# Projecting the later batches beside the attention heads, in one straight program

## What is computed

```python
Q, K, V = (proj(Wq, bq), proj(Wk, bk), proj(Wv, bv))        # [B, H, N, dh]
S = jnp.einsum('bhnd,bhmd->bhnm', Q, K) / dh ** 0.5
W_tau = jax.nn.softmax(S, axis=-1)
W_sigma = 1.0 / ((1.0 + jnp.abs(S) / b_) ** 2 + t_ ** 2)
W_sigma = W_sigma / W_sigma.sum(axis=-1, keepdims=True)
f = 0.5 * tau + 0.5 * sigma        # tau = W_tau @ V, sigma = W_sigma @ V, heads side by side
y = f @ Wo.T + bo
out = x + ln_w * (y - mu) * jax.lax.rsqrt(var + LN_EPS) + ln_b
```

## Time and profile before

| | before |
|---|---|
| median of 3 runs | 2139.07 us (2138.07 to 2139.43) |
| the profiled execution, its own time | 2139.67 us |
| its span, first to last instruction | 2137.9 us |
| granted TensorE clock, mean | 0.911 |
| first sigma scores of head 0 | 96.27 us |
| last instruction of attend_heads | 1699.8 us |
| PE busy | 1622.2 us (76%) |
| VectorE busy | 1888.1 us (88%) |
| ScalarE busy | 1577.8 us (74%) |
| GpSimd busy | 1609.9 us (75%) |

### The profile page before, as it was taken

One profiled execution on the slowest core, in us unless ns is written; L12 is line 12 of the kernel. 1 busy time (PEld: TensorE's weight loads), 2 busy tenths in 40 slices (PEclk: granted clock), 3 DMA queues, 4 the chain that ended last, 5 costly groups with the idle time before them and its releaser, 6 DMA issues. The chain is left out here.

```text
span 2137.9 us, 34185 instructions
## 1 busy us (share of the span) xinstructions
PE 1622.2 (76%) x8579; PEld 574.7 (27%) x8579; DVE 1888.1 (88%) x3699; ACT 1577.8 (74%) x1395; POOL 1609.9 (75%) x1198
## 2 busy tenths in 40 slices
PE   4477777878777778878777877777777668798976
PEld 2211222212211212222121212112221234366655
DVE  5799999999999999999999999999999378755556
ACT  3288889988888998989898998898998611122243
POOL 2399999999999999999999999999999321100000
PEclk9689999999999999999999999999999878877788
DMA  3300000000000000000000000000000000000001
GB/s 104 103 7 12 12 11 11 15 13 11 11 11 11 15 13 11 11 11 12 14 13 11 11 11 12 14 13 11 11 11 11 1 1 0 1 0 0 0 1 40
DMA packets 28864, 31.75 MB, mean 15 GB/s; under 512 B 5210, under 2 KB 16545, under 8 KB 28833
## 3 DMA queue, kind: packets, MB, share of 16 engines
q1 hardware_dynamic: 28832, 31.40, 4.9%
HBM read 22.74 MB, written 8.39 MB: 15 GB/s over the span
## 5 line engine op out<-in xcount | busy, mean ns | idle before, releaser
L837 POOL TENSOR_TENSOR sigma_weights<-grown 128x1024 f32<-128x1024 f32 x512 | 970.9, 1896 | 0.0
L709 DVE TENSOR_SCALAR sigma_weights<-ps_sig 128x512 int32<-128x512 int32 x1024 | 691.8, 676 | 24.1 <-PE ps_sig L608 19.5
L595 PE MATMUL ps_acc<-tau_weights,v_operand 128*9 128x512 f32 x2048 | 553.3, 620 | 96.1 <-ACT sigma_weights L761 89.4
L789 ACT ACTIVATE tau_weights<-ps_tau 128x1024 f32<-128x1024 f32 x512 | 514.3, 1004 | 149.1 <-PE ps_tau L626 148.7
L608 PE MATMUL ps_sig<-q_operand,k_operand 96*128 96x512 bf16 x1024 | 415.3, 406 | 261.0 <-DVE running_max L716 246.0
L716 DVE TENSOR_TENSOR running_max<-ps_sig,running_max 128x512 f32<-128x512 f32 x896 | 606.8, 677 | 0.0
L813 POOL TENSOR_SCALAR grown<-sigma_weights,shape_operand 128x1024 f32<-128x1024 f32 x512 | 575.7, 1124 | 39.2 <-DVE sigma_weights L709 38.9
L595 PE MATMUL ps_acc<-sigma_weights,v_operand 128*9 128x512 f32 x2048 | 555.3, 622 | 0.2 <-ACT sigma_weights L761 0.2
L755 ACT ACTIVATE sigma_weights<-sigma_weights,shape_operand 128x2048 f32<-128x2048 f32 x256 | 509.9, 1992 | 17.3 <-POOL sigma_weights L837 17.2
L761 ACT ACTIVATE sigma_weights<-sigma_weights 128x2048 f32<-128x2048 f32 x256 | 485.4, 1896 | 0.1
L626 PE MATMUL ps_tau<-q_operand,k_operand 128*128 128x512 bf16 x1024 | 314.9, 389 | 0.2 <-DMA q_operand<-max_rows 0.2
(11 more groups left out here) (171 smaller groups left out, 1489.5 us busy)
## 6 DMA issues: line engine op xcount, KB each, us to landing
q_operand<-q_parts SPq DMA_DIRECT2D x192, 48.0 KB
k_operand<-k_parts SPq DMA_DIRECT2D x64, 144.0 KB
q_parts<-parts SPq DMA_DIRECT2D x12, 256.0 KB, 2.9
k_parts<-parts SPq DMA_DIRECT2D x12, 256.0 KB, 3.0
x_res<-in_L_attn_x SPq DMA_DIRECT2D x4, 512.0 KB, 7.0
q_operand<-max_rows SPq DMA_DIRECT2D x128, 2.0 KB
out<-x_res SPq DMA_DIRECT2D x4, 512.0 KB, 3.2
experts<-in_L_ffn_expert_w SPq DMA_DIRECT2D x1, 512.0 KB
```

The costliest lines, as they stand in the source:

```text
L595: mm = pe.matmul(ps_acc[32 * q:32 * q + COLS, :], vop[:, (slot - 1 + kind) % SLOTS, j, :], weights[:, half * HALF:(half + 1) * HALF], star ...
L709: dve.tensor_scalar(sig[:, tile % SIG_RING, cols].bitcast(I32), ps_sig[:, half, :].bitcast(I32), SIGN_OFF, None, ALU.bitwise_and)\
L789: act.activation(tau[:, (head_slot * TB + of) % TAU_RING, :], ps_tau[:, of % 2, :, :].rearrange("p h q -> p (h q)"), ACT.Exp, scale=float( ...
L837: pool.tensor_tensor(sig[:, tile % SIG_RING, :], t, t, ALU.mult)\
```

## The change

- load_weights and project_heads are gone as blocks. Only batch 0 is projected first. Batches 1 to 3 are projected in pieces that the engines' orders name slot by slot, within the first 21 slots of the batch ahead (a class Beside runs each piece when its due slot is reached). Slots are counted through: 512 tiles plus 22.
- q and k are projected and split by halves of 512 tokens. parts holds one half; the next high part waits until the stores of the half before have landed. The high and middle parts are ScalarE's, rest is VectorE's (from PSUM, with the bias), the low parts are all GpSimd's.
- The projections need two PSUM banks (ps_side). ps_tau has one buffer instead of two: scores of a tile wait for the exponential of the tile before.
- The lags are PV_LAG 9 (7) and TAU_LAG 13 (12).
- v is read where it lies; the copies of v and shape constants on GpSimd are gone. ScalarE's step of max_rows is VectorE's.
- divide writes its quotient back to PSUM, and complete adds from there to the result. The result is kept by tokens, so that L952's copy is gone.
- ln_b is added to x beside the heads, and not in mix_experts.
- No hardware loops are left on GpSimd, TensorE and SP in the later blocks, nor in rounds.
- x is loaded by half batches, batches 2 and 3 after the operands of head 0; the first weights and biases are issued from ScalarE's queue.

```diff
-TAU_SHIFT = 4
+LOG_LAG, EXP_LAG = 5, 6
+PV_LAG = 9
+TAU_LAG = 13
...
+        ps_tau, ps_sig = ps("ps_tau", [P, 2, HALF]), ps("ps_sig", [P, 2, HALF])
+        ps_misc, ps_acc = ps("ps_misc", [P, HALF]), ps("ps_acc", [P, HALF])
+        ps_side = [ps(f"ps_side{i}", [P, HALF]) for i in range(2)]
...
+            def store_parts(b, g):
+                sp.wait_ge(low_ready, 4 * b + 2 * g + 2)
+                for s, scratch in enumerate((q_parts, k_parts)):
+                    for i in range(PARTS):
+                        sp.dma_start(scratch[b * H:(b + 1) * H, i, :, g * HALF:(g + 1) * HALF], parts[:, s, i, :])\
+                            .then_inc(stored, 16)
...
+                for b in range(B - 1):
+                    for g in range(2):
+                        yield b * BATCH_SLOTS + 13 + 6 * g
+                        store_parts(b + 1, g)
...
+            load_x(0)
+            load_x(1)
+            load_later()
+            for g in range(2):
+                store_parts(0, g)
+            sp.wait_ge(stored, 16 * 4 * PARTS)
+            for n in range(SLOTS):
+                load_operands(n)
...
+                n = (g - TAU_LAG) // TB - 1 + SLOTS
+                if (g - TAU_LAG) % TB == 0 and SLOTS <= n < NH:
+                    sp.wait_ge(tau_ready, (n - SLOTS) * TB + TB)
+                    if n % H == 0:
+                        sp.wait_ge(stored, 16 * 4 * PARTS * (n // H + 1))
+                    load_operands(n)
+                beside.upto(g)
...
+            def tau_scores(g):
+                head, of = g // TB, g % TB
+                if of == 0:
+                    pe.wait_ge(mrow_loaded, 32 * head + 32)
+                wait(pe, tau_done, g)
...
+                    yield t0 + (10, 11, 15.5, 16.2)[i]
+                    dve.wait_ge(hi_ready, 4 * b + i + 1)
+                    wait(dve, low_ready, 4 * b + i - 1)
+                    done(dve.scalar_tensor_tensor(out=rest[:, s, :], in0=bank(n)[:, :], scalar=(bq, bk)[s][:, 0:1],
+                                                  in1=parts[:, s, 0, :], op0=ALU.add, op1=ALU.subtract), n)
...
+                if of >= 1:
+                    dve.tensor_tensor(turned[:, :, 0:2, 0:DH], turned[:, :, 0:2, 0:DH], over(0), ALU.mult).then_inc(norm_step, 1)
...
+            def complete(of):
+                dve.wait_ge(norm_step, normed(of) + 2)
+                dve.tensor_tensor(result(of - 1), turned[:, :, 0:2, 0:DH], result(of - 1), ALU.add).then_inc(misc_done, 1)
...
+                    wait(act, stored, 16 * 2 * PARTS * (2 * b + g))
+                    act.activation(parts[:, s, 0, :], bank(n)[:, :], ACT.Identity, bias=(bq, bk)[s][:, 0:1]).then_inc(hi_ready, 1)
...
+                for i, at in ((2, 14.7), (3, 15.5)):
+                    yield t0 + at
+                    high(i)
...
+                    yield t0 + (11.5, 12.2, 17, 17.6)[i]
+                    pool.wait_ge(mid_ready, 4 * b + i + 1)
+                    pool.tensor_tensor(parts[:, s, 2, :], rest[:, s, :], parts[:, s, 1, :], ALU.subtract).then_inc(low_ready, 1)
...
+            for g in range(TILES):
+                if g + 1 < TILES:
+                    grow(g + 1)
+                beside.upto(g)
+                pool.wait_ge(grown_ready, g + 1)
+                t = grown[:, g % GROWN_RING, :]
+                pool.tensor_tensor(sig[:, g % SIG_RING, :], t, t, ALU.mult).then_inc(sq_ready, 1)
+                beside.upto(g + 0.5)
...
-                act.activation(f[:, :, :, :].rearrange("p t h d -> p h t d"), w["f"][:, bass.ds(b * H, H), :, :],
-                               ACT.Copy).then_inc(f_copied, 1)
```

More of the change, by code:

```diff
@@ L111, in build @@
         descend_tree(nc, w, out)
[L114 to L146, removed]
@@ L556, in _, with take, read, done @@
+            beside.upto(ALL)
         @block.tensor
         def _(pe):
-            def turn_running(slot, half, before):
-                wait(pe, misc_done, before)
+            def take(n):
+                wait(pe, side_read[n % 2], n // 2)
+            def read(n):
+                pe.wait_ge(side_read[n % 2], n // 2 + 1)
+            def done(mm, n):
+                mm.then_inc(side_ready[n % 2], 1)
+            def turn_four(n, tile_of):
+                take(n)
+                for t in range(4):
+                    mm = pe.transpose(bank(n)[:, t * P:(t + 1) * P], tile_of(t), ident[:, :])
+                done(mm, n)
@@ new lines, in side, with sigma_scores @@
+            def side():
+                for b in range(B - 1):
+                    yield from project(b + 1, b * BATCH_SLOTS)
+                    if b == 0:
+                        yield from prepare(PREPARE_AT)
+            def sigma_scores(g, half):
+                slot, keys = g // TB % SLOTS, slice(g % TB * P, (g % TB + 1) * P)
+                wait(pe, run_ready, 2 * g - 1 + half)
+                pe.matmul(ps_sig[:, half, :], kop[0:SIGMA_ROWS, slot, keys],
+                          qop[0:SIGMA_ROWS, slot, half * HALF:(half + 1) * HALF], start=True, stop=True).then_inc(sig_ready, 1)
@@ L592, in weigh @@
                     if kind in kinds:
-                        tile = slot * TB + j
-                        weights = tau[:, (tile - TB) % TAU_RING] if kind == 0 else sig[:, tile % SIG_RING]
-                        mm = pe.matmul(ps_acc[32 * q:32 * q + COLS, :], vop[:, (slot - 1 + kind) % SLOTS, j, :],
-                                       weights[:, half * HALF:(half + 1) * HALF],
-                                       start=(j == 0), stop=(j == TB - 1))
-                mm.then_inc(pv_done, 1)
@@ L644, in _ @@
-            stages(pe, stage)
-            turn_sums(NH, misc_before(NH + 1) + 1)
+                        weights = tau[:, (i - TB) % TAU_RING] if kind == 0 else sig[:, i % SIG_RING]
+                        mm = pe.matmul(ps_acc[32 * q:32 * q + COLS, :], v[:, (of - 1 + kind) % (2 * H), j, :],
+                                       weights[:, half * HALF:(half + 1) * HALF], start=j == 0, stop=j == TB - 1)
+                mm.then_inc(pv_done, 1)
+            beside = Beside(side())
+            pe.wait_ge(ident_step, 2)
@@ L1289, in _ @@
         def _(pool):
-            with pool.Fori(0, B) as b:
+            for b in range(B):
                 pool.wait_ge(z_ready, b * TB + TB)
@@ L1297, in _ @@
         def _(pe):
-            with pe.Fori(0, B) as b:
+            for b in range(B):
                 for t in range(TB):
@@ L1527, in _ @@
         def _(sp):
-            with sp.Fori(0, B) as b:
+            for b in range(B):
                 sp.wait_ge(x_done, b * 2 + 2)
```

1064 lines of the change are left out of this document (526 added, 538 removed).

## The result

The changed kernel takes 2085.66 us (median of 4 runs, 2084.50 to 2086.97), against 2139.25 (4 runs, 2138.07 to 2141.16) for the kernel before on the same chip: ratio 0.9749, 95% interval 0.9732 to 0.9766, or -53.6 us. The forecast was 2082.3, in a range of 2060 to 2122. The profiled execution took 2086.19, its span is 2084.4, its mean granted clock 0.927 (before 0.911).

The account below looks back on a forecast made before the run. GpSimd's two passes per tile were taken as the bound. Start, 1514.1 of squares, 29.5 pieces, 20 idle, 25 tail and small terms gave 1645.5 us; plus 437.6 - 2 made 2081.1, as a run 2082.3, range 2060 to 2122.

Parts of the forecast that it names:

- What bounds the kernel: Attention over heads: GpSimd's two passes per tile are the bound, squares 2.96 us apart; 511 steps make 1514.1 us.
- Part 1, the start: Before the first head: only one batch projected first, so first scores at 47 us instead of 96.3, bounds 42 and 54.
- Part 2, GpSimd's own work: Beside the heads: copies of 19.5 us removed, eight 128x512 instructions for each of three batches added, 29.5 us.
- Part 3, the operand in PSUM: Complete's stall goes with its second SBUF input, 35 us idle; rival that the wait stays, 2117, chance 0.05.
- Part 3, the idle time: GpSimd idle beside the heads: 6 us per batch, 18, plus 2 for the ramp, 20 in all; ends 0 and 45.
- The stall behind the stores: Second half's high part waits until first half's parts land; ScalarE stands some 9 us, 6 us idle GpSimd per batch.
- The part on the two new PSUM banks: Rival on ps_tau's one buffer: scores and exponentials wait for each other, 3.18 us a tile, 2173; chance 0.09.
- about covered: SyncE's queue: stores of slot 19 ahead of head 3's loads, 3.8 + 3.2 + 2.2 us against a short lead.
- a sign of being wrong: The prediction is wrong if TensorE waits at a head's first scores, or squares stand over 3.0 us apart away from pieces.
- the lead covers it: VectorE's shift keeps two SBUF inputs, may wait 5.2 us once a batch; ScalarE's h and TensorE's turning wait, no cost.
- The straight program: Hardware loops become straight code: 20 us gain if sequencers stalled 1 us at each of 20 loop ends; counted 0.
- Part 4, the end: After the last square: trailing exponentials and products 25 us, within 22 to 32; removing the f copy saves 2 us.

## Why the prediction was right, step by step

- **What bounds the kernel.** Right. Squares 2.96 us apart in both kernels; the kernels above in which a feeder's wait was removed gained about what GpSimd had been idle for it.
- **Part 1, the start.** Right to 2 us: first sigma scores at 44.85 instead of 47. h starts at 11.65 (12.1), ScalarE's second high part at 28.08, 16.4 behind h (18.9), the operand loads at 38.05. The first half could be stored 10.8 us after h started (12.7 forecast; the terms that the prediction lists for it add up to 13.3), and each set of stores landed 1.7 to 1.8 us after its issue instead of 2.4. The loads went the other way: first scores came 3.7 us after their last issue, not 2.2. No step was missing. The experiment with parts by half shows that the single buffer costs 5 us of it.

```profile
28.08 0.69 ACT L720 ACTIVATE parts<-ps_side,bq_col 128x512 bf16<-128x512 f32 x1 [7.04 <-DMA k_parts<-parts]
...
44.85 1.01 PE L407 MATMUL ps_sig<-q_operand,k_operand 96*128 96x512 bf16 x2 [11.47 <-DMA k_operand<-k_parts]
```

- **The first square** came 7.35 us after the scores (7.5 forecast).
- **Part 2, GpSimd's own work.** Right: 29.5 forecast; 12 low parts at 1.12 and 12 additions at 1.23 from start to start are 28.2. The squares' term was 1514.1; 511 x 2.958 = 1511.5.
- **Part 3, the operand in PSUM.** Right, and shown twice. The Trainium skill (GPSIMD Engine Reference, Key points) gives two SBUF inputs as a cause of contention; the runs agree (2586 and 214 ns for the same sum). The neighbour rest (L541), with one input in PSUM, never exceeds 0.75 us in 16 times.
- **Part 3, the idle time.** This is the mis-sized term: 20 forecast, 31.6 found. The stall behind the stores has the place and chain foretold, 6.43 per batch against 6; that the size fits is partly luck, since ScalarE stood 5.8 to 7.7 us and not 9. The ramp, forecast at 2, left 0.3. The other 12.3 us are, but for 0.6 in two small gaps (the ramp's among them), three waits, of which the prediction named two and priced both at nothing:
  - TensorE's matmuls of q and k at slots 10 and 11 wait for PSUM banks, ahead of the next tau scores: some 3.4 us in each of batches 2 and 3, 6.7 in all. The part on the two new PSUM banks went no further than ps_tau; the question who waits behind a waiting instruction was put to SyncE, ScalarE and VectorE, but not to TensorE's new pieces.
  - SyncE's stores ahead of head 3's loads, "about covered": TensorE waits 5.01, 3.74 and 4.17 us at this head's first scores, which the prediction had named as a sign of being wrong. GpSimd's lead covers it in batches 2 and 3; in batch 1 it costs 2.05 us, at 136 and 141 us.
  - The shift, "the lead covers it": it took 5.08 us in batches 2 and 3, and 1.5 and 1.4 us of gaps follow it (467 and 471 us above). The prediction named ScalarE's h and TensorE's turning as its waiters; in the trace TensorE's scores stand first (4.85 us, behind the running maximum), then ScalarE's exponential (4.42), and h after that. The last link shows: TensorE's turning waits 1.13 us for h, ahead of the next scores, and VectorE's magnitude 1.15. No run was made to take the shift's wait away, but two traces have it short by chance: in the kernel with the product in SBUF it took 0.31 and 0.30 us in batches 2 and 3 (463.13 and 868.61), in the changed kernel's batch 1 0.80 (57.71), and in none of these three do the gaps follow 16 and 20 us behind it.

```profile
464.80 0.66 PE L343 MATMUL ps_side<-ident,h 128*128 128x128 f32 x4 [1.13 <-ACT h L692]
466.15 0.69 DVE L565 TENSOR_SCALAR sigma_weights<-ps_sig 128x512 int32<-128x512 int32 x1 [1.15 <-PE ps_sig L407]
```

- **The straight program.** Counted at 0. The kernel before with only complete changed keeps its loops and has the same 2.96 us a tile and 3.8 us of idle time, all of it ahead of the first squares, so in this stage there was nothing to gain. The stall at taken branches that the Trainium skill (Runtime: NRT & Kernel Launch, Instruction fetch mechanics) tells of has no visible price there. The loops of the later blocks, the two longer lags and the missing f copy were not tried alone.
- **Part 4, the end.** From the last square's end (1625.2) to the next stage (1649.83) 24.6 us, 25.5 forecast (25 and the 0.5 of the stage's start). With one ps_tau buffer the trailing exponentials wait for scores, the last one 0.95 us. From there to the end 434.6, against 437.6 - 2 = 435.6 forecast.

```profile
1642.92 1.02 ACT L777 ACTIVATE tau_weights<-ps_tau 128x1024 f32<-128x1024 f32 x1 [0.95 <-PE ps_tau L416]
...
1649.32 0.23 DVE L618 TENSOR_TENSOR f_tokens<-ps_misc,f_tokens 128x64 f32<-128x64 f32 x1
1649.83 1.28 ACT L973 ACT_TABLE_LOAD   x1 [5.89 <-PEq L162]
```

So the span missed by 3.3 us (2081.1 against 2084.4), of which +11.6 are idle time, and -8.3 the start (2.3), the squares (2.8), the pieces (1.3) and the end (1.9). The closeness of the sum is partly that of errors of opposite sign.

## What to carry to other kernels

Where VectorE and GpSimd both look full, look for VectorE instructions whose duration varies although their size doesn't, and for their second SBUF input: moving one operand of 128x64 to PSUM was worth 37 to 40 of the 54 us, and everything else in this change only the rest. When work is slotted beside a bound engine, ask of every new piece, on every engine and queue, what it waits for and what stands behind it; a buffer per half was worth 24 us, one matmul's slot 7.5. And the price of work on the bound engine is only its duration while its feeders have a lead: the same six additions were worth 0 to 2 us with a late DMA behind them and 5.8 without. When a removal brings too little, look for the next late transfer before giving the sum up.

## What the runs showed of the hardware

VectorE's shift writes 128x8, with both inputs in SBUF. It took 0.17 us at the start, where GpSimd stood idle, and 5.08 beside the squares of two batches:

```profile
450.43 5.08 DVE L521 SCALAR_TENSOR_TENSOR shift<-mean_var,rstd 128x8 f32<-128x8 f32 x1
...
451.44 1.11 POOL L835 TENSOR_SCALAR grown<-sigma_weights,kernel_shape 128x1024 f32<-128x1024 f32 x1
452.52 1.88 POOL L860 TENSOR_TENSOR sigma_weights<-grown 128x1024 f32<-128x1024 f32 x1
454.39 1.11 POOL L835 TENSOR_SCALAR grown<-sigma_weights,kernel_shape 128x1024 f32<-128x1024 f32 x1
```

It did not end when the running GpSimd instruction ended at 451.4, nor after the next two, but with the fourth, at 455.5. So the wait need not be for one instruction of the other engine: with GpSimd's back to back it lasted through four, for an instruction that takes 0.17 us by itself. It need not be long either. In batch 1 the shift met a grow and ended with it, and so it did in the kernel with the product in SBUF (the first pair of lines is the changed kernel's, the second that kernel's):

```profile
57.38 1.12 POOL L835 TENSOR_SCALAR grown<-sigma_weights,kernel_shape 128x1024 f32<-128x1024 f32 x1
57.71 0.80 DVE L521 SCALAR_TENSOR_TENSOR shift<-mean_var,rstd 128x8 f32<-128x8 f32 x1
...
462.31 1.12 POOL L836 TENSOR_SCALAR grown<-sigma_weights,kernel_shape 128x1024 f32<-128x1024 f32 x1
463.13 0.31 DVE L522 SCALAR_TENSOR_TENSOR shift<-mean_var,rstd 128x8 f32<-128x8 f32 x1
```

The 64 completes of the kernel before say the same in larger number. The three that found GpSimd not running took 0.22 to 0.23 us. Each of the other 61 ended 0.06 to 0.09 us after the end of some GpSimd instruction: 25 after the first that ended, 11 after the second, 13 after the third, 11 after the fourth and one, of 7.26 us, after the seventh. With the product in SBUF in the changed kernel it was 43 after the first and 18 after the third, 0.22 to 4.80 us. Nothing had to stand idle for that: the one at 945.59, in the head that the prediction reads as meeting a gap, took 0.63 us and ended with a running grow. What decides which end it is no run shows.
